# Base of the output written before the experts, shared sums added in five pieces, wide experts' tiles in another order, 16-bit group comparison

## What is computed

```python
x = x + gnn(layernorm(x), edges)              # segment sum over 10625 edges, two linear layers with batch norm and relu
h = layernorm(x)
shared = sum(silu(h @ sWg[e]) * (h @ sWu[e]) @ sWd[e] for e in range(2))
top_w, top_i = top_k(softmax(h @ Wr), 6)      # of 64 experts, weights divided by their sum
routed = sum(silu(h @ Wg[e]) * (h @ Wu[e]) @ Wd[e] * gate[:, e] for e in range(64))
out = x + (shared + routed + h)
```

## Time and profile before

| | before |
|---|---|
| median of three runs | 781.27 us |
| the profiled execution | 782.4 us |
| its span, first to last instruction | 780.7 us |
| mean granted TensorE clock | 0.981 |
| TensorE busy | 722.4 us (93%) |
| VectorE busy | 260.5 us (33%) |
| ScalarE busy | 195.1 us (25%) |
| GpSimd busy | 174.7 us (22%) |
| DMA | 236.35 MB, mean 303 GB/s |

### The profile page before, as it was taken

How to read it: one execution, slowest core, us unless ns; L and a number is a source line. 1 busy time by engine, 2 the same in 40 slices (tenths; PEclk the granted TensorE clock), 3 DMA queues, 4 the chain that set the end, 5 groups by cost and what they waited for, 6 DMA issues and landing times. The chain is left out here.

```text
span 780.7 us, 17521 instructions
## 1 busy us (share of the span) xinstructions
PE 722.4 (93%) x7096; PEld 478.5 (61%) x7096; DVE 260.5 (33%) x788; ACT 195.1 (25%) x497; POOL 174.7 (22%) x157
## 2 busy tenths in 40 slices
PE   2699999879999999999999999999999999489993
PEld 2597776556666666555566666655566666356662
DVE  7983524975221442222221212121233222012100
ACT  1222321402332222211222222121222333033331
POOL 4000000011222232232332222222333332123211
PEclk9999999999999999999999999999999999789996
DMA  9970021426999999999999999999999999999921
GB/s 265 407 280 3 0 108 62 166 75 222 354 341 337 347 387 382 392 392 380 385 387 390 378 401 377 384 394 389 383 384 372 373 374 368 342 369 364 337 36 23
DMA packets 57265, 236.35 MB, mean 303 GB/s; under 512 B 6171, under 2 KB 6335, under 8 KB 40286
## 3 DMA queue, kind: packets, MB, share of 16 engines
q1 hardware_dynamic: 46004, 211.33, 70.8%
q0 software_dynamic: 10144, 20.56, 11.4%
q10 hardware_dynamic: 1034, 3.30, 1.1%
HBM read 222.32 MB, written 12.83 MB: 301 GB/s over the span
## 5 line engine op out<-in xcount | busy, mean ns | idle before, releaser
L424 POOL DMA_INDIRECT xg<-x_tab,idx_sb x64 | 71.8, 1121 | 387.9 <-DVE idx_sb L942 220.0
L1368 PE MATMUL ps<-ring,xT 128*64 128x256 f32 x1296 | 156.5, 383 | 0.6 <-ACT xT L608 0.6
L439 POOL DMA_INDIRECT out<-ysb,idx_sb x64 | 92.5, 1445 | 202.4 <-DMA out<-ysb,idx_sb 124.4
L1368 PEld LDWEIGHTS ps<-ring,xT 128*64 128x64 f32 x1296 | 88.1, 137 | 43.8 <-issue 3.4
L628 ACT ACTIVATE ysb<-ps 64x256 f32<-64x256 f32 x64 | 24.2, 377 | 332.3 <-PE ps L1368 152.5
L935 DVE TENSOR_REDUCE gates<-ps 128x1 f32<-128x3 f32 (+1 forms) x62 | 10.0, 162 | 267.7 <-PE ps L1275 267.0
L1368 PE MATMUL ps<-ring,hTj 128*64 128x256 f32 x624 | 75.5, 384 | 0.0
L1368 PE MATMUL ps<-w,xT 128*64 128x256 f32 x608 | 75.1, 390 | 0.0
L903 DVE TENSOR_TENSOR onehot<-iotaAB,slotv 125x640 bf16<-125x640 f32 (+1 forms) x64 | 67.3, 1051 | 2.6 <-PE ps L1283 1.8
L999 DVE SCALAR_TENSOR_TENSOR hs<-hs,gates,ps 128x256 f32<-128x256 f32 x64 | 30.7, 480 | 90.2 <-PE ps L1373 43.8
L1368 PEld LDWEIGHTS ps<-ring,hTj 128*64 128x64 f32 x624 | 42.1, 136 | 30.1 <-issue 11.9
(11 more groups left out here) (237 smaller groups left out, 818.2 us busy)
## 6 DMA issues: line engine op xcount, KB each, us to landing
ring<-in_L_ffn_Wg SPq DMA_DIRECT2D x41, 1024.0 KB, 20.7
ring<-in_L_ffn_Wu SPq DMA_DIRECT2D x40, 1024.0 KB, 21.2
ring<-in_L_ffn_Wd SPq DMA_DIRECT2D x39, 1024.0 KB, 22.5
w<-in_L_ffn_Wd SPq DMA_DIRECT2D x20, 1024.0 KB, 22.4
w<-in_L_ffn_Wg SPq DMA_DIRECT2D x19, 1024.0 KB, 21.6
w<-in_L_ffn_Wu SPq DMA_DIRECT2D x19, 1024.0 KB, 21.3
ring_x<-in_L_ffn_Wu SPq DMA_DIRECT2D x5, 1024.0 KB, 20.2
ring_x<-in_L_ffn_Wd SPq DMA_DIRECT2D x5, 1024.0 KB, 20.3
```

The costliest lines, as they stand in the source:

```text
L424: g.indirect_dma_start(out=xg[j % NX][0:ROWS[j], :], out_offset=None, in_=x_tab, in_offset=bass.IndirectOffsetOnAxis(ap=idx_sb[0:ROWS[j], ...
L439: g.indirect_dma_start(out=out, out_offset=bass.IndirectOffsetOnAxis(ap=idx_sb[0:ROWS[j], j:j + 1].bitcast(u32), axis=0), in_=ysb[h][0:ROW ...
L1368: last = t_.matmul(ps[h * BIG:(h + 1) * BIG, bank, 0:AW], big(k), w[:, k, h * AW:(h + 1) * AW], start=(k == 0), stop=(k == KD - 1))
```

## The change

Six edits.

1. The zero fill is gone. SP writes `x_sb` (the base) to `out` before item 13, `s_base0` tells of it, and the first scatter waits for it. Then `x_sb` is free: the first shared expert's down products are copied into it, the second one's added. `add_shared` adds one tile of 125 rows to `out` after each of the scatters 41, 45, 49, 53 and 57, as DMAs of 112 and 13 rows.
2. `one_m` is made from two 16-bit tensors: `iota_m` has all 625 columns, and ScalarE spreads `col_m` to 16-bit `rep` buffers (`spread`), ten of them. Six lie where ring buffer 7 is, so item 7 waits for the last comparison.
3. Wide experts but the first run as `gate_and_up`: big gate, big up, small gate, small up. Their down product runs small tiles first.
4. All down weights are loaded as 4 KB rows. So h of wide experts is laid out with even and odd columns apart too: silu and mult work on rearranged columns, h needs four transposes, and h_copy three instructions.
5. The last block's sum is added to `hT` by VectorE instead of copied by ScalarE.
6. The order of the last block and the loop for more rounds is turned round on TensorE.

```diff
-    BASE_AFTER = 50
-    PRE = 3 * 16
+    SHARED_AFTER = [41, 45, 49, 53, 57]
+    NREP = 10
...
+                if i == 7:
+                    sp.wait_ge(s_sm, NG)
...
+                if i == 13:
+                    for a, b in PARTS:
+                        sp.dma_start(out.rearrange("(t p) d -> p t d", p=P)[a:b, :, :], x_sb[a:b, :, :]).then_inc(s_base0, 16)
...
-                if r == 2 and CAPS[j] == BIG:
+                if r == 2:
...
-                if j == BASE_AFTER + 1:
-                    pool.wait_ge(s_base, 32)
+                if j == 0:
+                    pool.wait_ge(s_base0, 32)
+                if j - 1 in SHARED_AFTER:
+                    pool.wait_ge(s_base, 32 * (SHARED_AFTER.index(j - 1) + 1))
...
+            def add_shared(t, j):
+
+                pool.wait_ge(s_sy, (NS - 1) * T + t + 1)
+                pool.wait_ge(s_scat[0], (j + 2) // 2 * 16)
+                pool.wait_ge(s_scat[1], (j + 1) // 2 * 16)
                 for a, b in PARTS:
-                    g.dma_start(out.rearrange("(t p) d -> p t d", p=P)[a:b, :, :], x_sb[a:b, :, :],
-                                accum_op=ALU.add).then_inc(s_base, 16)
+                    g.dma_start(out[t * P + a:t * P + b, :], x_sb[a:b, t, :], accum_op=ALU.add).then_inc(s_base, 16)
...
+            def spread(b):
+                for g in range(b * GB, (b + 1) * GB):
+                    if g >= NREP:
+                        act.wait_ge(s_sm, g - NREP + 1)
+                    sc.activation(rep[g % NREP][:], col_m[:, g * U:(g + 1) * U].unsqueeze(2).broadcast_to([P, U, P]),
+                                  ACT.Copy).then_inc(s_rep, 1)
...
-                sc.activation(hTj[:, 0:wide], ps[:, 2, 0:wide], ACT.Copy).then_inc(s_hc, 1)
+                last = sc.activation(hTj[:, 0:AW], ps[:, 2, 0:AW], ACT.Copy)
+                if wide > AW:
+                    odd_even = ps[0:BIG, 2, AW:2 * AW].rearrange("p (b h r t) -> p r h b t", b=2, h=2, r=2)
+                    for r in range(2):
+                        last = sc.activation(hTj[r * BIG:(r + 1) * BIG, AW:HW].rearrange("p (h b t) -> p h b t", h=2, b=2),
+                                             odd_even[:, r, :, :, :], ACT.Copy)
+                last.then_inc(s_hc, 1)
...
+                    last = v.tensor_tensor(one_m[slot][:], iota_m[:], rep[g % NREP][:], ALU.is_equal)
...
+                    if e == 0:
+                        v.tensor_copy(x_sb[:, t, :], ps[0:P, 5, :]).then_inc(s_sy, 1)
...
+            def tiled(bank, big, small, w, done):
+
                 if small is not None:
-                    for k in range(KD):
-                        for q in range(4):
-                            last = t_.matmul(ps[q * SMALL:(q + 1) * SMALL, bank, AW:HW], small(k),
-                                             w[:, k, q * 128:(q + 1) * 128], start=(k == 0), stop=(k == KD - 1))
-                last.then_inc(done, 1)
+                    small_tiles(bank, small, w)
+                big_tiles(bank, big, w).then_inc(done, 1)
+
+            def gate_and_up(x, w_gate, w_up, j):
+                big_tiles(0, lambda k: x[:, k, 0:BIG], w_gate())
+                if j >= 1:
+                    pe.wait_ge(s_mul, j)
+                big_tiles(1, lambda k: x[:, k, 0:BIG], w_up())
+                small_tiles(0, lambda k: x[:, k, BIG:CAP], w_gate()).then_inc(s_g, 1)
+                small_tiles(1, lambda k: x[:, k, BIG:CAP], w_up()).then_inc(s_u, 1)
```

## The result

The changed kernel took 794.92 us (median of four runs, 793.72 to 796.78), the kernel before on the same chip 782.43. The ratio is 1.0156, with a 95% interval from 1.0115 to 1.0198: slower, 12.5 us.

What follows compares the result with a forecast made beforehand. TensorE was taken as busy but for a 17.6 us stall from GpSimd's add, with a nearly slackless scatter chain. Span 780.7 + 10.8 + 1.4 = 792.9; the same 12.2 on the 781.27 median gave 793, range 771 to 804.

Steps and rivals of the forecast that it cites:

- The stall: TensorE near 680 us: the 17.6 us loss goes; waits of 4 to 10 us near 600, 640 and 720 replace it.
- The price of an add: GpSimd's 125-row adds: each lands in 8.8 us, 9.7 with its pause, 48.5 for five; bounds 3.9 and 18.5.
- line through scatters and big add: Landing times of 80- and 96-row scatters (8.4 us) and 560 add rows (17.3): 0.019 us a row, 8.9 for 125.
- The chain: Scatters 41 to 58, each waiting for the one before: 176.9 us less 21.4 plus 48.5, 204.0 as an upper figure.
- the 9 us: Taken off scatters 41 to 58 as DMA catches up with weights: 0.55 us for each of 16 landings.
- first five wide slots: Experts 1 to 5, ahead of scatter 41: 0.4 to 0.5 us slower each, 2.2 us in all.
- The tail: Scatter 58 lands at 763.2 and holds up the copy of expert 60, 14.7 us later than before; 10.8 reach TensorE.
- 3.9 of reserve: Between wide down products near the end: 3.9 us of lateness of ScalarE's copy to ysb cost TensorE nothing.
- Order of the wide experts: Gate and up together: 0.4 us gained in shapes, 0.3 lost to transposes, 0.6 waiting for h; net 0.4 to 0.5 slower.
- late slots' loss: The sixteen late wide experts' slower order: mostly hidden behind the scatters; only the last three add 1.4 us.
- 4 KB runs: Down weights loaded as longer rows: TensorE waits for no weights after 166 us, so zero effect.
- Graph stage: VectorE from 22.6 to 52.5 us: 20 compares on 16-bit inputs gain 3.0 us, between ends of 0 and 6.0.

Runs made afterwards that it cites:

- seventh experiment: Changed kernel, complete with its five adds, with three ysb buffers instead of two: 788.94 us, ratio 1.0081 against the kernel before.
- fourth experiment: Changed kernel without its adds (shared sums missing), gate and up of wide experts run apart again: 769.21 us, ratio 0.9824 against the kernel before.
- twelfth experiment: Changed kernel, complete with its five adds, with gate and up of wide experts run apart: 794.92 us, ratio 1.0147 against the kernel before.
- third experiment: Changed kernel with one add of all 625 rows after scatter 50 in place of the five: 789.60 us, ratio 1.0088 against the kernel before.
- sixth experiment: Changed kernel with gate and up apart, one add after the last scatter, wide down weights in 2 KB rows (routed sums wrong): 777.26 us, ratio 0.9934.
- eighth experiment: Kernel before with its one add of 625 rows moved from scatter 50 to behind the last scatter: 778.36 us, ratio 0.9937.
- tenth experiment: Changed kernel with one add after scatter 62, last graph block ahead of the branch, small halves of h copied first: 772.10 us, ratio 0.9863.
- second experiment: Changed kernel with the five adds after scatters 58 to 62: 789.32 us, ratio 1.0092 against the kernel before.
- first and fourth experiments: Changed kernel without its adds: 776.21 us with gate and up together (first), 769.21 us with them apart (fourth).
- experiments 5 and 8: One 625-row add behind the last scatter: in the changed kernel with gate and up apart (5), 774.27 us; in the kernel before (8), 778.36 us.
- experiments 9 to 11: Changed kernel, one add after scatter 62, last graph block before the branch: gate and up apart 775.95 us (9), plus third ysb buffer 774.94 us (11).

## Why the prediction was right

**The stall.** The 17.6 us did go, and waits took their place at the buffers, near 587, 631, 680 and 726 us where I had said 600, 640 and 720 (4 to 10 us each; measured 3.7 to 7.9).

**The price of an add.** Issue of the first DMA to landing of the last was 9.2, 9.9, 8.5, 8.9 and 4.6 us, against 8.8 from the line through scatters and big add. The fifth met few weights. The steps with an add were 18.0, 18.7, 19.4, 18.9 and 14.0 us.

**The chain.** From scatter 41 to 58 I had 204.0 less 9, which is 195.0; the trace has 195.2 (564.55 to 759.73). In its parts that is luck. I had spread the 9 us evenly, 0.55 for each of 16 landings. The first four steps with an add gave 0.4 in all, the fifth 4.8 (14.0 where I had 18.8), and the twelve without an add 3.6 (8.85 us each instead of 9.15). The seventh experiment fits a chain that goes at its own pace: a third buffer took 7.4 us off TensorE's waits and only 3.4 off these 195.2. I started the chain at 562.2, 2.4 us too early: the graph stage gave 2.8 less and slot 1 lost 1.6 at the lower clock (both below), while the first five wide slots cost 0.9 instead of 2.2 (3.1 by these terms, 2.4 measured). The span (794.9 against 792.9) came out 2.0 above the sum.

**The tail.** Here the path that I had drawn was not the one, though the number came near. I let scatter 58, behind the fifth add, hold up the copy of expert 60 and TensorE behind it. ScalarE's timeline in the changed kernel, first at expert 56, then at expert 60:

```profile
726.63 0.38 ACT L653 ACTIVATE ysb<-ps 64x256 f32<-64x256 f32 x1 [9.56 <-DMA out<-ysb,idx_sb]
...
764.97 0.38 ACT L653 ACTIVATE ysb<-ps 64x256 f32<-64x256 f32 x1 [3.67 <-DMA out<-ysb,idx_sb]
...
768.43 0.49 ACT L636 ACTIVATE hs<-ps 128x384 f32<-128x384 f32 x1 [1.57 <-PE ps L1409]
```

The copy of expert 60 did run at 764.97 (763.2 predicted, 748.49 in the earlier trace rows), 3.67 us late. But the silu behind it then still waited 1.57 us for TensorE, so that lateness cost nothing. What held up TensorE last was scatter 54, issued at 718.62 behind the *fourth* add: the copy of expert 56 stood 9.56 us for its landing, and the down product of expert 57 started at 729.84. From there TensorE went at its own pace, with the wide down products at 741.26, 751.10, 760.94 and 770.78. So the fifth add cost TensorE nothing in this trace.

The 14.2 us of the span are then: 13.0 by which that down product is later than before (716.86), 2.9 from slower tiles behind the wait and longer slots up to the last product, less 1.3 in the last scatters and 0.3 in the closing instruction. I had reached 12.2 by the copy of expert 60, less 3.9 of reserve, plus 1.4. That the two agree to 2 us is in part luck: the chain and TensorE end within 1.6 us of each other.

**Order of the wide experts.** The sign was right, the size not: 0.18 us more a slot (9.66 in the earlier trace rows, 9.84 now) instead of 0.45. By its terms: the wait was 0.5 for 0.6. Without it the slot would be 9.34, 0.32 under 9.66, where I had a gain of 0.4 in shapes less 0.3 for the transposes. The four transposes take 0.49 us (659.81 to 660.30); the three of before took some 0.4. So I priced the narrow transposes' shape changes too high by about 0.2, and the changes of shape in the products were worth what I said (0.32 and 0.1 are 0.42). The rule on mode changes in the Trainium skill ("TensorEngine Tiling (Array Packing)", section "Key Properties") agrees with this as far as it goes; the fourth experiment shows what it doesn't see, the 0.5 us of lost cover, which outweighed it.

I had the late slots' loss mostly hidden behind the chain. The twelfth experiment leaves open how much of it is. With one add it isn't hidden: the third experiment is 6.6 us over the kernel before. With the five adds and the old order of gate and up the time is 11.9 us over the kernel before (twelfth, 794.9 against 783.05, some 3 of it the hole); with both changes 12.5, less than the sum of the two.

**4 KB runs.** Priced at nothing. The sixth experiment points to some 3 us of gain from them where the chain is near its limit, within the noise of two overlapping intervals. If it is real, this term was wrong by that much, in the harmless direction.

**Graph stage.** This is the term of the sum that missed most. Of 3.0 us, 0.2 arrived in the profiled execution: the first product of the linear layer started at 63.22 instead of 63.38. The compares did their part. VectorE from 22.6 to 52.5 us:

```profile
L729 DVE TENSOR_TENSOR one_s<-iota_s,col_s 125x625 bf16<-125x625 int16 x20 | 16.1, 806 | 0.0
L732 DVE TENSOR_TENSOR one_m<-iota_m,rep 125x625 bf16<-125x625 int16 x20 | 9.6, 481 | 0.0
```

481 ns instead of 816, 0.335 us less each. The estimate by the Trainium skill, "VectorE: DVE Perf Modes", section "What auto-detection actually checks", was 0.33; the trace agrees with the rule there that a two-tensor operation goes at double rate when every tensor is 16-bit. The 6.7 us less of VectorE made TensorE the bound, and it reached the end of the fourth block 3.3 us earlier. What came then had no term in my sum, the turned order (edit 6). TensorE in the changed kernel:

```profile
49.58 4.68 PE L1153 MATMUL ps<-aT,h 125*128 125x125 f32 x40
56.05 6.33 PE L1153 MATMUL ps<-aT,h 125*128 125x125 f32 x40 [1.79 <-issue]
63.22 3.17 PE L1212 MATMUL ps<-hT,w 128*128 128x313 f32 x11 [0.84 <-DVE hT L826]
```

The branch for more rounds, not entered, now stands between two products and opens a pause of 1.79 us; before, a wait for ScalarE's copy covered it in part (1.33). And the last block took 6.33 us instead of 4.68, because the granted clock was at its lower level from 57.4 to 60.8 us (0.81 on the mean from 57 to 66). That drop was not in any of the other traces (granted clock 1.00 from 54 to 62 us in all twelve experiments): with the same code the linear layer began at 60.7 to 62.3 us there (eight traces), and with the last block ahead of the branch at 59.8 to 60.9 (three). So 3.0 us was the right size for the compare and its place; turned round, it is about 2, and in the profiled execution the clock took the rest.

Slot 1 lost another 1.6 us to the lower clock (TensorE, 172 to 178 us):

```profile
172.79 1.37 PE L1409 MATMUL ps<-ring,xT 128*32 128x128 f32 x32
174.09 3.29 PE L1402 MATMUL ps<-ring,xT 128*64 128x256 f32 x16
```

Small tiles take 1.37 instead of 1.01 to 1.08, big ones 3.29 instead of 1.95. The gap ahead (1.66 us, then 0.35) is the same in the kernel before, whose profile kept the full clock there; in the eighth experiment, which has its code, the clock fell at this place too (0.74 on the mean from 170 to 174 us). Of all the traces only those of the kernel before and of the tenth experiment keep 1.00 there. So this can't be charged to the change.

## What to carry to other kernels

When work is cut into pieces to shorten a stall, first ask which serial chain each piece joins, and multiply the piece's latency, not its bytes: five adds of 125 rows put 42.5 us into a chain (five steps of 89.0 us in all, less five of 9.3) in which one of 625 had put 21.4, though they hold the same data. Then ask up to where that chain still holds the engine: here the last of the five adds held up nothing, since TensorE was by then later than the chain. In the second experiment all five stood in the tail and cost there as well (TensorE's last product waited 6.5 us). And an order that saves changes of shape must be read together with what it uncovers: put the wait that it exposes behind the shortest part of the copy (tenth experiment).

## What the runs showed of the hardware that I had not expected

- The instruction that closes GpSimd's program took 10.5 us in the first and fourth experiments, whose expert stage has only gathers and scatters on GpSimd, and 1.0 to 1.8 us in the kernels with an add. Anyone who measures a DMA by leaving it out must look at what comes last. The cause wasn't tried.
- A large add behind one of the last two scatters starts late: 3.5 us after the landing in experiments 5 and 8, where behind scatter 50 it was 0.6. Small adds in the same tail don't show it (scatter 62 landed at 774.18, add at 774.71). Whether this and the closing instruction are one thing is open.
- A branch over a loop that isn't entered left TensorE 1.4 to 1.8 us without work between two products that otherwise follow each other without a gap. Behind the last block (experiments 9 to 11) it showed as a wait of 1.3 to 1.45 us where 0.84 stands without it.
- The same order of tiles ran with a hole of 0.28 us in the small tiles, 0.8 to 0.9 us a slot, in four early slots of three kernels (9, 11, 12), and without it in three others (4, 5, 6).
- The clock's drop behind the same short gap (1.66 us, then 0.35) came in 12 of 14 traces, in the kernel before's code both with and without it.
